# A third weight group as four quadrant matmuls ahead of the convolution stream, in other PSUM banks

## The reference, cut to what matters

```python
def _qlinear(x, W, b):
    y = q_acc(jnp.einsum('bsk,nk->bsn', q_mul(x), q_mul(W)))   # q_mul: 5/2-bit float, q_acc: 5/10-bit float
    return q_acc(y + q_mul(b))
...
x = x + _L0_conv_ref(_ln_c(x), ...)          # 3x3 conv of 12 channels, 1x1 in, 8x8 FFT weights, gelu gate, 1x1 out
t = _to_tokens(x)                            # 48 channels per token
h = jax.nn.relu(_qlinear(_ln_t(t), W1, b1))  # 48 -> 192, the first layer
y = _qlinear(h, W2, b2)                      # 192 -> 48, the second layer
x = _from_tokens(t + y, x)
```

## Time and profile before

| | |
|---|---|
| device time, median of 3 | 694.96 us |
| the profiled execution, its own time | 693.84 us |
| its span, first to last instruction | 692.0 us |
| TensorE busy | 662.4 us, 96% |
| VectorE, ScalarE, GpSimd busy | 86%, 77%, 66% |
| mean granted TensorE clock | 0.987 |

### The profile page before, as it was taken

How to read it: one execution, slowest core, us unless ns; L and a number is a source line. 1 busy time by engine, 2 the same in 40 slices (tenths; PEclk the granted TensorE clock), 3 DMA queues, 4 the chain that set the end, 5 groups by cost and what they waited for, 6 DMA issues and landing times.

```text
span 692.0 us, 19152 instructions
## 1 busy us (share of the span) xinstructions
PE 662.4 (96%) x6608; PEld 526.0 (76%) x6608; DVE 595.5 (86%) x1159; ACT 534.6 (77%) x1086; POOL 458.5 (66%) x348
## 2 busy tenths in 40 slices
PE   5889999999999999999999999999999999999984
PEld 4667778877787788777877887778778877787851
DVE  6658798899989888999898889988988899877887
ACT  4234588888888888888888988888889888777784
POOL 4535667786777777876777778767767887653353
PEclk9999999999999999999999999999999999999995
DMA  4544445554445455544444555444545554342102
GB/s 103 108 101 122 108 102 132 143 140 108 121 122 144 105 136 142 141 117 115 122 122 124 138 142 135 118 117 125 143 118 124 139 142 116 92 121 76 46 24 69
DMA packets 52207, 80.73 MB, mean 117 GB/s; under 512 B 20823, under 2 KB 36079, under 8 KB 52111
## 3 DMA queue, kind: packets, MB, share of 16 engines
q1 hardware_dynamic: 49903, 78.17, 43.9%
q10 hardware_dynamic: 2208, 1.34, 0.8%
HBM read 63.17 MB, written 16.30 MB: 115 GB/s over the span
## 4 chain that ended last, share of the span: by engine, by line
PE 81%; DMA 7%; DVE 3%; issue 3%; SPq 2%; POOL 2%; ACT 1%; DVEq 0%; POOLq 0%; ACTq 0%
PE inva L537 16%; PE invb L544 14%; PE mixp L524 12%; PE misc L553 8%; PE misc L813 7%; PE misc L624 4%; PE misc L524 4%; DMA taps<-cz_scratch 3%; PE misc L668 3%; PE misc L775 3%; PE misc L573 2%; PE misc L582 2%; DMA cz_scratch<-cz 2%; PE misc L658 2%; PE mixp L637 2%
## 5 line engine op out<-in xcount | busy, mean ns | idle before, releaser
L1594 POOL TENSOR_TENSOR st<-st,neg_half 128x16 f32<-128x16 f32 x32 | 93.3, 2915 | 106.6 <-DVE st L1498 106.6
L537 PEld LDWEIGHTS inva<-inv,gmix 128*127 128x127 f32 x1024 | 123.3, 190 | 25.3 <-DVE gmix L1270 13.2
L537 PE MATMUL inva<-inv,gmix 128*127 128x128 f32 x1024 | 141.0, 280 | 0.6 <-DVE gmix L1270 0.6
L1270 DVE TENSOR_TENSOR gmix<-mixp,freq_w 128x508 f32<-128x508 f32 x192 | 122.5, 679 | 16.6 <-PE mixp L524 16.6
L544 PE MATMUL invb<-inv,gmix 128*127 128x128 f32 x1024 | 134.7, 274 | 0.1
L544 PEld LDWEIGHTS invb<-inv,gmix 128*127 128x127 f32 x1024 | 126.1, 191 | 2.1 <-DVE hbuf L1281 0.5
L906 ACT ACTIVATE hid<-misc 128x512 f16<-128x512 f32 x180 | 94.1, 599 | 17.7 <-PE misc L624 17.7
L1626 POOL TENSOR_TENSOR st<-st,neg_half 128x16 f32<-128x16 f32 x31 | 95.5, 3080 | 16.4 <-DVE st L1349 16.4
L1281 DVE TENSOR_TENSOR hbuf<-gact,invb 127x512 f32<-127x512 f32 x128 | 87.3, 682 | 21.6 <-ACT gact L898 16.7
L898 ACT ACTIVATE gact<-inva 127x512 f32<-127x512 f32 x128 | 77.5, 605 | 21.9 <-PE inva L537 21.3
L915 ACT ACTIVATE hid<-hid 128x512 fp8e5<-128x512 f16 x174 | 93.2, 619 | 0.0
(11 more groups left out here) (185 smaller groups left out, 1332.3 us busy)
## 6 DMA issues: line engine op xcount, KB each, us to landing
taps<-cz_scratch SPq DMA_DIRECT2D x63, 292.2 KB
xres<-in_x_dram SPq DMA_DIRECT2D x64, 192.0 KB, 4.1
xin<-in_x_dram SPq DMA_DIRECT2D x62, 192.0 KB, 3.5
out_dram<-ob SPq DMA_DIRECT2D x60, 192.0 KB, 2.6
taps<-cz_scratch SPq DMA_DIRECT2D x63, 146.1 KB
crm<-rm_scratch SPq DMA_DIRECT2D x58, 96.0 KB
cx<-in_x_dram SPq DMA_DIRECT2D x32, 96.0 KB
cz_scratch<-cz SPq DMA_DIRECT2D x63, 48.8 KB
```

Source lines behind the costliest of these rows:

```text
L537: mm = pe.matmul(inva[0:HID, q * PX:(q + 1) * PX], gmix[:, s % 2, q, 0:HID], inv[:], start=True, stop=True, skip_group_check=True)
L1270: dve.tensor_tensor(gmix[:, s % 2, 2 * q:2 * q + 2, 0:HID2], pair[q][:, 0:2 * HID2].rearrange("p (e c) -> p e c", e=2), freq_w[:], ALU.mul ...
L1594: pool.tensor_tensor(st1[:, 6, :], st1[:, 5, :], neg_half[:], ALU.pow).then_inc(pow1, 1)
```

## The change

The first layer's third group is no longer one block-diagonal matmul per half. Behind the whole of `inverse(t, 3, 1)`, ahead of `stream`, four matmuls are issued (`hidden_rest`), each 48 rows by 64 outputs by 512 columns, one for each pair of half c and band j. Row half j of the array and column half c: they lie in the four quadrants. Band 1 of both halves goes to bank 0, band 0 of both halves to bank 2. So `hid16` and `hid8` hold, in order: groups 0 and 1 of half 0, the rest of band 1, the rest of band 0 (each with half 0 in partitions 0 to 63 and half 1 in 64 to 127), groups 0 and 1 of half 1. Groups 0 and 1 of half 1 land in banks 1 and 0. `hidden_rest` first waits until ScalarE has copied group 0 of half 0 out of bank 0.

The second layer reads the new layout with as many matmuls (8), in another order: its wait for the sixth conversion stands behind the second matmul, not behind the sixth. ScalarE makes the same six copies, as 0 and 1, then the gelu, then one of bank 0 (new index 2), in steps 3 to 5 `rm_t`, the convolution's copy, then three more. VectorE makes three ReLUs of 2 x 512 columns in place of two of 2 x 512 and two of 512; one stands where relu(t, 0) did, two where relu(t, 1) did. In steps 3 to 5 `rows` stands behind `hidden_rest` on TensorE. In the drain the item left over from step 34 is read in the new layout (`older_half`), waiting for four conversions in place of three; the last two items go as before.

```diff
+            def hidden_rest(t):
+                pe.wait_ge(hid16_ready, upto(6 * at(t, 5) + 1))
+                for c in range(2):
+                    for j in (1, 0):
+                        r0 = HALF * j
+                        mm = pe.matmul(bank[0 if j else 2][HALF * c:HALF * c + HALF, :], l1h[r0:r0 + CH, 2, r0:r0 + HALF],
+                                       q16[r0:r0 + CH, 4 * c:4 * c + 4, :], start=True, stop=True,
+                                       skip_group_check=True)
+                        if c == 1:
+                            mm.then_inc(hid_done, 1)
...
+            def rest_product(dst, c, j):
+                r0, o = HALF * c, HALF * j
+                return pe.matmul(dst[o:o + HALF, :], l2[:, 2, r0:r0 + HALF], hid8[:, (3, 2)[j], :],
+                                 start=False, stop=True, skip_group_check=True)
...
                 for c in range(2):
-                    for g in range(2):
-                        r0 = HALF * g
-                        pe.matmul(pair[c][r0:r0 + HALF, :], l2[:, g, r0:r0 + HALF], hid8[:, 3 * c + g, :],
-                                  start=True, stop=False, skip_group_check=True)
-                for c in range(2):
                     if c == 1:
                         pe.wait_ge(hid8_ready, upto(6 * l + 6))
                         pe.sem_inc(pe_held, 1)
-                    for r0 in (0, HALF):
-                        mm = pe.matmul(pair[c][r0:r0 + HALF, :], l2[:, 2, r0:r0 + HALF], hid8[:, 3 * c + 2, :],
-                                       start=False, stop=True, skip_group_check=True)
+                    for g in range(2):
+                        r0 = HALF * g
+                        pe.matmul(pair[c][r0:r0 + HALF, :], l2[:, g, r0:r0 + HALF], hid8[:, 4 * c + g, :],
+                                  start=True, stop=False, skip_group_check=True)
+                for c in range(2):
+                    for j in range(2):
+                        mm = rest_product(pair[c], c, j)
                     mm.then_inc(y_done, 1)
...
-                def last_group():
-                    if live(t, 0) and 3 <= a < ROWS_EARLY:
-                        rows(t, 0)
-                    if live(t, 5):
-                        pe.wait_ge(tsq_ready, upto(2 * m + 1, 2 * STEPS))
-                        hidden(t, 0, 2, bank[2])
-
-                if live(t, 3):
-                    inverse(t, 3, 1, last_group)
-                else:
-                    last_group()
+                if live(t, 3):
+                    inverse(t, 3, 1)
+                if live(t, 5):
+                    pe.wait_ge(tsq_ready, upto(2 * m + 2, 2 * STEPS))
+                    hidden_rest(t)
+                if live(t, 0) and 3 <= a < ROWS_EARLY:
+                    rows(t, 0)
...
                     pe.wait_ge(hid16_ready, upto(6 * k + 2))
-                    hidden(t, 1, 0, bank[0])
-                    hidden(t, 1, 1, bank[1])
+                    hidden(t, 1, 0, bank[1])
                     pe.wait_ge(hid16_ready, upto(6 * k + 3))
-                    hidden(t, 1, 2, bank[2])
+                    hidden(t, 1, 1, bank[0])
...
                 if live(t, 5):
-                    accumulators(t, 0, (0,))
+                    accumulators(t, (0, 1))
+                if live(t, 3):
+                    gelu(t, 3, 1)
+                if live(t, 5):
+                    accumulators(t, (2,))
                 if live(t, 0) and 3 <= a < ROWS_EARLY:
                     rows(t, 0)
-                if live(t, 5):
-                    accumulators(t, 0, (1, 2))
-                if live(t, 3):
-                    gelu(t, 3, 1)
...
-            def relu(t, c, parts=((0, 2), (2, 1))):
+            def relu(t, i):
                 k = at(t, 5)
-                for g, size in parts:
-                    dve.wait_ge(hid16_ready, upto(6 * k + 3 * c + g + size))
-                    buf = hid16[:, 3 * c + g:3 * c + g + size, :]
-                    dve.tensor_scalar(buf, buf, bq[:, g // 2:g // 2 + 1], 0.0, ALU.add, ALU.max)\
-                       .then_inc(relu_ready, size)
+                dve.wait_ge(hid16_ready, upto(6 * k + 2 * i + 2))
+                buf = hid16[:, 2 * i:2 * i + 2, :]
+                dve.tensor_scalar(buf, buf, bq[:, i % 2:i % 2 + 1], 0.0, ALU.add, ALU.max).then_inc(relu_ready, 2)
```

More of the change, by code:

```diff
@@ L697, in first_layer, with older_half @@
                         hidden(t, c, g, dst[g])
+                def older_half(c, dst):
+                    for g in range(2):
+                        r0 = HALF * g
+                        pe.matmul(dst[r0:r0 + HALF, :], l2[:, g, r0:r0 + HALF], hid8[:, 4 * c + g, :],
+                                  start=True, stop=False, skip_group_check=True)
+                    for j in range(2):
+                        mm = rest_product(dst, c, j)
+                    mm.then_inc(y_done, 1)
                 def second_layer_half(c, dst):
@@ L711, in drain @@
                 pe.wait_ge(h_ready, 4 * NEW + 2)
+                pe.wait_ge(hid16_ready, 6 * OLDER + 3)
                 project_half(0, bank[3])
                 def between():
-                    pe.wait_ge(hid8_ready, 6 * OLDER + 3)
-                    second_layer_half(0, mixp[0])
+                    pe.wait_ge(hid8_ready, 6 * OLDER + 4)
+                    older_half(0, mixp[0])
                 inverse(t, 4, 3, between)
@@ L727, in drain @@
                 pe.wait_ge(y16_ready, 2 * OLDER + 1)
-                second_layer_half(1, mixp[0])
+                older_half(1, mixp[0])
                 pe.wait_ge(tpix_ready, 2 * NEW + 1)
@@ L769, in turn_x @@
                 if FIRST <= t[1] < LAST:
-                    pe.wait_ge(hid16_ready, upto(6 * l + 5))
+                    pe.wait_ge(hid16_ready, upto(6 * l + 6))
                 elif a == 0:
@@ L898, in gelu, with accumulators, activations @@
                 act.activation(gact[:, s % 2], inva[0:HID, :], ACT.Gelu).then_inc(gelu_ready, 1)
-            def accumulators(t, c, groups):
+            def accumulators(t, groups):
                 k = at(t, 5)
                 for g in groups:
-                    act.wait_ge(hid_done, upto(6 * k + 3 * c + g + 1))
-                    act.wait_ge(hid8_ready, upto(6 * (k - 1) + 3 * c + g + 1))
-                    act.activation(hid16[:, 3 * c + g, :], bank[g][:], ACT.Copy).then_inc(hid16_ready, 1)
-            def activations(k, c, groups):
+                    act.wait_ge(hid_done, upto(6 * k + g + 1))
+                    act.wait_ge(hid8_ready, upto(6 * (k - 1) + g + 1))
+                    act.activation(hid16[:, g, :], bank[(0, 1, 0, 2, 1, 0)[g]][:], ACT.Copy).then_inc(hid16_ready, 1)
+            def activations(k, groups):
                 for g in groups:
-                    act.wait_ge(relu_ready, upto(6 * k + 3 * c + g + 1))
-                    if c == 0 and g == 0:
+                    act.wait_ge(relu_ready, upto(6 * k + g + 1))
+                    if g == 0:
                         act.wait_ge(y_done, upto(2 * k))
                     act.sem_inc(act_held, 1)
-                    act.activation(hid8[:, 3 * c + g, :], hid16[:, 3 * c + g, :], ACT.Copy, saturate=False)\
+                    act.activation(hid8[:, g, :], hid16[:, g, :], ACT.Copy, saturate=False)\
                        .then_inc(hid8_ready, 1)
@@ L1000, in convert @@
                     act.wait_ge(relu_ready, 6 * k + 3 * c + g + 1)
-                    act.wait_ge(y_done, 2 * (k - 1) + c + 1)
+                    act.wait_ge(y_done, 2 * (k - 1) + (c + 1 if k == NEW else 2))
                     act.activation(hid8[:, 3 * c + g, :], hid16[:, 3 * c + g, :], ACT.Copy, saturate=False)\
@@ L1114, in step @@
                 if live(t, 6):
-                    activations(l, 0, range(3))
-                    activations(l, 1, range(3))
+                    activations(l, range(6))
                 if live(t, 6):
@@ L1144, in step @@
                 if live(t, 5):
-                    accumulators(t, 1, range(3))
+                    accumulators(t, (3, 4, 5))
                 if live(t, 2):
@@ L1410, in convert @@
                     dve.wait_ge(relu_ready, 6 * k + 3 * c + g + 1)
-                    dve.wait_ge(y_done, 2 * (k - 1) + c + 1)
+                    dve.wait_ge(y_done, 2 * (k - 1) + (2 if k == OLD else c + 1))
                     dve.tensor_copy(hid8[:, 3 * c + g, :], hid16[:, 3 * c + g, :], saturate=False).then_inc(late_hid8, 1)
@@ L1533, in step @@
                     relu(t, 1)
+                    relu(t, 2)
                 if live(t, 3):
```

## The result

| | before | changed |
|---|---|---|
| median of 20 executions each | 693.80 us | 695.41 us |
| ratio of the times | | 1.0028 [1.0016, 1.0041] |
| the profiled execution, its own time | 693.84 us | 696.16 us |
| its span | 692.0 us | 694.3 us |
| its mean granted TensorE clock | 0.987 | 0.983 |

The forecast time was 695.4. The forecast difference was +0.4 us. The medians differ by +1.6; the ratio, taken without one execution of the kernel before that took 1693.0 us, says 0.28%, or +1.9 us, with an interval of 1.1 to 2.8.

What follows compares the result with a forecast made beforehand. TensorE was taken as the bound, working without a break from step 4 on. +1.39 (step 3), +0.75 (step 6) and -1.7 (steady steps) sum to +0.4 us, forecast 695.4 us; 8-in-10 range 692.9 to 697.8.

Steps and rivals of the forecast that it cites:

- rival 3: Row tables' delay hidden or smaller and shape changes cheaper with quadrants: 691.5 us, half of that 693.2; chance 0.14.
- Quadrants, one slot; a change between tiled shapes 0.11: Around the inverse, four quadrants share one 0.22 us slot and the change to the stream's shape adds 0.11.
- The second place: At half 1, pair, shape change and L582 take 0.81 us in place of 0.98, 0.17 shorter.
- Steady steps: Steps 6 to 34 each get 0.06 us shorter, -1.7 us over 29 steps.
- Waits (a) to (e): Possible new waits in the steady step, on copies, conversions and inputs; all together put at nothing.
- (b) and (c): Half 1's group 1 waiting for index 2's copy, and `convolve` for a copy 0.1 later; both put at nothing.
- Step 3, +1.39: Row table's copy starts 1.39 us later, delaying the taps and step 4's stream one to one.
- Step 4: Its row table gets 0.88 us later, in time for a TensorE 1.39 behind: no cost.
- Step 5 "comes out even": Step 5 itself has one shape change more and was to cost nothing; its table comes 2.97 us late.
- Step 6, +0.75: Step 5's late table delays the last taps load, so step 6's stream stands still 0.75 us, range 0 to 1.5.
- The drain, 0: At the end, the older item's half waits for four conversions, not three: 0, at most 0.3 us either way.
- rival 2: Clock falls in step 4's longer standstill, costing 1.5 to 2 us: 697.2 us; chance 0.07.

Runs made afterwards that it cites:

- kernel 5: kernel 2 with the quadrants issued behind the stream and index 2's copy behind the convolution's on ScalarE: 693.88 us, ratio 1.0001.
- experiment 7: The changed kernel with one step's row table back between the inverse's halves: step 5's alone 695.62 us, 1.0010; step 3's alone 693.94 us, 0.9993.
- kernel 2: The changed kernel with the row tables of steps 3 to 5 back between the inverse's halves: 694.22 us, 0.9987; second run 692.60 us, 0.9974.
- kernel 6: Filler matmuls in TensorE's standstills, added to the changed kernel or kernel 2; with eight ahead of step 4's stream in the changed kernel: 696.53 us, 1.0018.
- kernel 1: The changed kernel run a second time, no edit: 697.37 us, ratio 1.0037.
- kernel 3: The kernel before, with only the row tables of steps 3 to 5 moved as the change moves them: 698.01 us, ratio 1.0047.
- two-filler kernel: kernel 2 with six filler matmuls ahead of step 4's stream and seven ahead of step 2's: 691.67 us, ratio 0.9947.
- kernel 4: kernel 2 with the four quadrant matmuls issued twice in a row: 699.12 us, ratio 1.0077.

## Why the prediction was right, and where it was not

A budget in stretches that start and end with the convolution's stream separates the steps. The first row's changed value is from the kernel with step 5's table back, since the first profile has a fall of the clock in that stretch; what it does up to step 4 is the change. In the first profile itself the stretch took 38.05, +4.0, of which 2.7 are the fall; with the other rows, and a stream of step 2 that starts 0.4 earlier, that is the +2.3 between the two spans.

| stretch | before | changed | difference | forecast |
|---|---|---|---|---|
| stream of step 2 to 4 | 34.04 | 35.42 | +1.4 | +1.39 |
| step 4 to 6 | 39.02 | 40.24 | +1.2 | +0.9 |
| step 6 to 33 | 533.10 | 531.04 | -2.1 | -1.6 |
| step 33 to the end of the span | 50.08 | 49.63 | -0.4 | -0.1 |
| sum | | | +0.1 | +0.6 |

(The forecast's +0.9 holds the 0.14 of two changes that the prediction named on TensorE's way to step 6 and left out of its sum of +0.4. Its 692.9, too, was called half of rival 3, which is 693.2.)

- **Quadrants, one slot; a change between tiled shapes 0.11.** Right, and for the reason given: 0.33 from quadrants to stream, and 0.22 for another round of four.
- **The second place, 0.98 to 0.81.** Right: 332.89 - 332.09 = 0.80, for 0.98 before.
- **Steady steps.** 0.05 a step (19.78 to 19.73), 1.4 us in 27 steps, for 0.06 and 1.6. The other 0.6 of the -2.1 are steps of 20.10, 20.04 and 19.82 in the profile of before, its own late taps in the earlier trace rows, of which the changed kernel's profile happened to have none.
- **Waits (a) to (e).** None shows up. (b) and (c) have little room: with the copies one place later (kernel 5) the pair waits 0.04.
- **Step 3, +1.39.** Right in its mechanism, and near in size. The stretch from the stream of step 2 to that of step 4 is 34.04 in the profile before, but 34.38 to 34.64 in four other traces whose table of step 3 was not moved, since the landing differs; so the move costs 0.8 to 1.4 there. The split was wrong: 0.57 of it comes ahead of the stream of step 3, where TensorE waits for the copy.
- **Step 4, no cost.** It held in the changed kernel. In the two kernels of experiment 7 the stream of step 5 waits 1.3 to 1.6 for its taps, most of it by landings of 5.24 and 6.53; whether the late table has a part in it is open.
- **Step 5 "comes out even".** This is the step that failed. I followed who waits for the table on SyncE and GpSimd and missed that TensorE waits too, at the very next group. My own times had it: TensorE through with the transpose near 89.1, the copy near 89.9. The row of step 5 shows 0.82 idle, and the stretch from step 4's stream to step 5's is 20.51 where kernel 2's second run, with the quadrants and the tables in their old place, has 19.36: 1.2 longer. The other 0.3 is not taken apart.
- **Step 6, +0.75.** In the changed kernel's profile no wait is shown: the 0.82 of step 5 has put TensorE that much later, and 4.77 us were left from the last load to the stream, just enough. It was 1.15 in kernel 6's version with eight fillers, which also waits 0.82 in step 5. There the last load was issued 16.39 us behind the copy of step 5's table and not 15.46, and took 5.01 to land, so both waits come one after the other, and step 4 to 6 takes 112.20 - 70.73 = 41.47, 2.4 more than before. By the prediction's own list of signs, a step 6 without a wait for the taps counts against it: the +1.2 of the second row comes near the forecast +0.9 because one wait, of 0.82 in step 5, stands in for another, of 0.75 in step 6. That is luck too.
- **The drain, 0.** It was 0.4 shorter, 0.1 of it the steady gain.
- **The clock.** Not in the sum, rival 2 at 0.07. The trace's budget gives +0.1 where +1.6 (and +2.8 in kernel 1) was measured. The mean granted clock over all executions is 0.9855 for the kernel before (92 executions) and 0.9837 for the changed one (32). A straight line through the executions gives 1.4 us for 0.0025 of mean clock, so this difference is about 1.1 us. At equal clock the line puts the changed kernel 0.1 to 0.3 above before, and kernel 2 2.1 below. This is an estimate, and likely too high for the clock's part: the mean also holds the half clock of the end, which lasts 15.4 us in the profile before and 17.1 in the changed kernel's, where the last stretch nevertheless got shorter. So the sum was right to about a microsecond, and what was measured above it goes in good part with the clock.

What is not settled is why the changed kernel has the lower clock. Part of it may be chance: the longest falls, 6.8 us behind the stream of step 2 (first profile, kernels 1 and 2), lie where TensorE's order is the same in all these kernels. For the longer standstill of step 4 speaks that in kernels 1, 2 and 3 the clock fell right behind it (1.86, 1.88, 2.46), and that behind the 1.16 of before it did not. Against it speaks that it did not fall behind 1.87 in the first profile of the change nor behind 1.95 in the kernel with step 5's table back; that filling this standstill alone did not bring the mean back; and that kernel 2's own mean was 0.9838 in one set and 0.9852 in the other, so that a set of 12 executions scatters by most of the difference in question. With steps 2 and 4 both filled the profile shows no fall before the end, and none of the 12 executions has a mean clock under 0.987. Step 4 alone was tried and did not do it; step 2 alone was not tried, and neither were fillers in the kernel before, so how much they would bring there is open.

Of the two-filler kernel's 0.53%, 3.7 us, kernel 2 has 1.8 without fillers in the same set, near the 1.4 to 1.7 of the quadrants' steady steps; the other 1.9 came with the fillers and the clock that no longer falls.

## What to carry to other kernels

Price a repacking by slots: a 512-column group saved brings 0.22 us here, each new border between tiled shapes costs half of that or a little more, so a change that saves one group and adds one border wins little. When an instruction moves in one engine's order, list every wait on what it produces, the same engine's next group among them, and do it for the few first steps that have an order of their own; three moved transposes cost about 3 us here, more than 29 steps of packing won. Where a kernel's executions spread by more than the edit is worth, read the granted clock of each and try to fill the standstills ahead of its falls, with a filler shorter than the standstill.

## What the runs showed of the hardware

- Equal standstills did not have equal consequences. Ahead of step 2's stream TensorE waits about 2 us in most profiles. Behind 1.87 (kernel 2), 2.06 (the changed kernel) and 2.23 (kernel 1) the granted clock fell to 1.2 GHz; behind 1.93 (kernel 2's second run), 1.94 (kernel 5), 2.03 (kernel 3) and 2.17 (kernel 4) it stayed at 2.4 GHz.
- Falls of the clock had different prices. Behind the stream of step 4 one cost 1.5 us (21.97 for 20.51), and the longer one behind the stream of step 2 cost 2.7 (18.17 for 15.46). One at 28 to 32 us, ahead of a wait for the taps, cost little: the stream of step 2 started at 35.15 to 35.76 in the three traces that have it and at 34.91 to 35.57 in the others.
- The last taps load took between 4.36 and 6.53 us from the start of its issue to landing on the chains of these kernels in steps 4 to 6 (among them 4.36, 4.66, 4.88, 4.95, 5.01, 5.24, 5.80, 6.53), with the same bytes each time. Steps 4 to 6 have less room than this spread, so which of their streams waits changes from kernel to kernel.
- Four 48 x 64 matmuls of 512 columns started within 10 ns of one another and took the slot of one.
